# Second layer of a four-part network on one Trainium2 core: when a block's first sums are issued, when the residual is added, and where the picks' places are summed

## What is computed

```
x = x + _L0_attn_ref(_layernorm(x), ...)   # decayed attention, then a feed-forward
x = x + _L0_ffn_ref(_layernorm(x), ...)    # 2 shared and 16 routed experts, top 4
x = x + _L1_attn_ref(_layernorm(x), ...)   # selective scan: the part changed here
x = x + _L1_ffn_ref(_layernorm(x), ...)    # 2 x 32 experts, top 2 of each
```

```
def step(h, inp):
    x_t, dt_t, B_t = inp
    dA = jnp.exp(dt_t[:, :, None] * A[None])
    h = dA * h + dt_t[:, :, None] * B_t[:, None, :] * x_t[:, :, None]
    y_t = h.sum(-1) + D[None, :] * x_t
    return (h, y_t)
...
y = y * jax.nn.silu(res)
return y @ W_out.T
```

## Time and profile before

| what | value |
|---|---|
| median of 3 runs | 4823.72 us |
| the profiled execution's own time | 4822.83 us |
| its span, first to last instruction | 4821.0 us |
| first layer alone, to about | 2200 us |
| the scans of the second layer, from about | 2500 us |
| to about | 4145 us |
| a chunk of 64 scans, chunks 1 to 14 | 101.8 to 106.3 us |
| sorted experts, from about | 4207 us |

### The profile page before, as it was taken

One profiled execution on the slowest core, in us unless ns is written; L12 is line 12 of the kernel. 1 busy time (PEld: TensorE's weight loads), 2 busy tenths in 40 slices (PEclk: granted clock), 3 DMA queues, 4 the chain that ended last, 5 costly groups with the idle time before them and its releaser, 6 DMA issues. The chain is left out here.

```text
span 4821.0 us, 59211 instructions
## 1 busy us (share of the span) xinstructions
PE 4269.6 (89%) x19350; PEld 2845.4 (59%) x19350; DVE 3709.2 (77%) x5917; ACT 2521.4 (52%) x4939; POOL 3002.8 (62%) x1908
## 2 busy tenths in 40 slices
PE   5689999999999999998989988989989988599993
PEld 1345566555566555565656566666556666488883
DVE  6887777787778787776128999988999989555677
ACT  1343334344334344333458777777877777255552
POOL 3445545465545455554147888888888889655552
PEclk7899999999999999999999999999999999699997
DMA  4233323333333333332121122121122122596887
GB/s 145 83 105 105 110 88 104 107 104 107 108 96 97 110 99 112 105 102 85 54 85 49 67 78 99 71 74 67 71 82 99 69 69 71 180 254 196 266 278 279
DMA packets 304193, 545.54 MB, mean 113 GB/s; under 512 B 31504, under 2 KB 148496, under 8 KB 294928
## 3 DMA queue, kind: packets, MB, share of 16 engines
q1 hardware_dynamic: 275664, 465.56, 30.0%
q0 software_dynamic: 27648, 75.67, 4.4%
q10 hardware_dynamic: 576, 0.53, 0.1%
HBM read 422.72 MB, written 118.92 MB: 112 GB/s over the span
## 5 line engine op out<-in xcount | busy, mean ns | idle before, releaser
L1528 POOL TENSOR_TENSOR c_dbx<-c_dtx,c_Brep 128x1024 f32<-128x1024 f32 x512 | 1203.0, 2363 | 159.2 <-DVE c_hs L1546 119.0
L876 POOL TENSOR_TENSOR a_kv<-a_rk,a_kv 128x512 f32<-128x512 f32 x512 | 807.3, 1589 | 404.4 <-DMA a_kv<-v_rows 404.2
L1546 DVE TENSOR_TENSOR_SCAN c_hs<-psum,c_carry,c_dbx 128x512 f32<-128x512 f32 x768 | 934.6, 1263 | 56.3 <-ACT psum L1535 41.7
L885 DVE TENSOR_TENSOR_SCAN a_S<-a_decay,a_carry,a_kv 128x513 f32<-128x513 f32 x512 | 792.6, 1548 | 181.6 <-POOL a_kv L876 93.3
L802 POOL TENSOR_TENSOR a_hid_e<-a_hid_e,a_g_rep 128x512 f32<-128x512 f32 x256 | 387.1, 1514 | 772.7 <-ACT a_hid_e L791 590.4
L1535 ACT ACTIVATE psum<-c_dt,c_cols 128x512 f32<-128x512 f32 x1024 | 695.2, 688 | 285.6 <-DVE c_hs L1546 283.6
L1571 PEld LDWEIGHTS psum<-ident,c_hs 128*128 128x128 f32 x4096 | 491.9, 145 | 343.2 <-DVE c_hs L1546 169.7
L1571 PE MATMUL psum<-ident,c_hs 128*128 128x128 f32 x4096 | 596.6, 282 | 87.3 <-DVE c_hs L1546 85.1
L891 DVE TENSOR_TENSOR a_prod<-a_rk,a_S 128x512 f32<-128x512 f32 x512 | 546.4, 1067 | 71.9 <-PE psum L907 71.8
L783 PE MATMUL psum<-a_W_down,a_hid_e 128*128 128x256 f32 x2304 | 550.8, 385 | 54.0 <-POOL a_hid_e L802 29.7
L207 PE MATMUL psum<-a_xT,a_W_up 128*128 128x512 f32 x1152 | 559.5, 616 | 14.7 <-ACT a_hid_e L791 14.6
(11 more groups left out here) (287 smaller groups left out, 6817.4 us busy)
## 6 DMA issues: line engine op xcount, KB each, us to landing
a_kv<-v_rows SPq DMA_DIRECT2D x512, 256.0 KB
a_g_rep<-g_rows SPq DMA_DIRECT2D x256, 256.0 KB, 3.9
c_Brep<-b_rows SPq DMA_DIRECT2D x64, 1024.0 KB, 6.0
d_xs<-sorted_rows SPq DMA_DIRECT2D x320, 128.5 KB
d_w<-results SPq DMA_DIRECT2D x64, 512.0 KB, 11.4
d_w<-in_d_experts SPq DMA_DIRECT2D x32, 768.0 KB
a_xa<-in_L_attn_x SPq DMA_DIRECT2D x16, 512.0 KB, 4.7
v_rows<-a_rv SPq DMA_DIRECT2D x16, 512.0 KB, 3.0
```

Source lines behind the costliest of these rows:

```text
L876: m_kv[g] = pool.mark(nc.gpsimd.tensor_tensor(kv[:, g % NV, 1:C + 1], rk[slot][:, 1, hb, :], kv[:, g % NV, 1:C + 1], ALU.mult))
L885: m_scan[q] = dve.mark(nc.vector.tensor_tensor_scan(S[:, q % NS, :], decay[cq % 2][:, hb, :], kv[:, q % NV, :], carry[:, sq_:sq_ + 1], ALU ...
L1528: m_dbx[g] = m_dbx[g + 1] = pool.mark(nc.gpsimd.tensor_tensor(dbx[:, r:r + 2, :], dtx[slot][:, e, :].unsqueeze(1).broadcast_to([P, 2, C]), ...
L1546: m_scan[q] = dve.mark(nc.vector.tensor_tensor_scan(hs[:, q % NR, :], psum[:, DA + q % ND, :], dbx[:, q % NX, :], first, ALU.mult, ALU.add))
```

## The change

Three edits, all in `layer1_phase`.

1. The skip term of a block and the sums of its first state are no longer issued in the first state's step but, together with the second state's sums, one step later (`sum_up(q - 1)`, then `sum_up(q)`). What `background.pull()` puts into PE's queue in the step between now stands ahead of them.
2. The pause ahead of the residual's addition grows from `LAG + 2` to `LAG + 6`, 4 yields more, at 1.2 a step some three steps. All that follows in `after_scan` moves by as much, to some four or five steps where it crosses other pauses.
3. The places of the picks are reduced into the PSUM bank that holds the ranks, behind them (`in_room`), and the cast reads them there. The bank comes free with the cast (L1394), not with the multiplication (L1386). The tile `place` is gone.

```diff
-                yield from pause(LAG + 2)
+                yield from pause(LAG + 6)
...
-            ranks = bank[:, 0:TL * NE]
+            ranks, in_room = bank[:, 0:TL * NE], bank[:, TL * NE:TL * NE + TL * Z.picks]
...
-            m = G.freed[i] = dve.mark(nc.vector.tensor_tensor(
+            m = dve.mark(nc.vector.tensor_tensor(
                 at_pick[:, :, :, :], R["onehot"][:, :, :, :],
...
-            m = dve.mark(nc.vector.tensor_reduce(flat(place[:, :, :, :].rearrange("p t g k -> p t (g k)")), at_pick[:, :, :, :].rearrange("p r s e -> p (r s) e"), AX, ALU.add))
+            m = dve.mark(nc.vector.tensor_reduce(in_room, at_pick[:, :, :, :].rearrange("p r s e -> p (r s) e"), AX, ALU.add))
             yield
             dve.after(m)
-            m_done["placed", c] = [dve.mark(nc.vector.tensor_copy(flat(route.to_row[:, c % 2, :, :]), flat(place[:, :, :, :].rearrange("p t g k -> p t (g k)")))), m_xn]
+            m = G.freed[i] = dve.mark(nc.vector.tensor_copy(flat(route.to_row[:, c % 2, :, :]), in_room))
+            m_done["placed", c] = [m, m_xn]
...
+            def sum_up(q):
+
+                cq, sq = divmod(q, steps)
+                e, n = divmod(sq, N)
+                if n == 0:
+                    pe.after(m_done.get("y free"))
+                    for t in range(TL):
+                        nc.tensor.matmul(psum[:, YB, t * P:(t + 1) * P], xs[cq % 2][:, e, t * P:(t + 1) * P], skip_diag[:, e, :],
+                                         start=(t == 0), stop=False, skip_group_check=True)
+                pe.after(m_scan[q])
+                for t in range(TL):
+                    last = nc.tensor.matmul(psum[:, YB, t * P:(t + 1) * P], hs[:, q % NR, t * P:(t + 1) * P], ident[:, :],
+                                            is_transpose=True, start=False, stop=(n == N - 1 and t == TL - 1), skip_group_check=True)
+                m_sum[q] = pe.mark(last)
...
-                    if n == 0:
...
-                    m_sum[q] = pe.mark(last)
+                    for at in ((q - 1, q) if n == 1 else (q,) if n else ()):
+                        sum_up(at)
```

More of the change, by code:

```diff
@@ L1563, in scans @@
                         m_kept[q] = act.mark(nc.scalar.copy(carry[:, e, n - 3:n + 1], hs[:, r - 3:r + 1, C - 1]))
-                    if n == 0:
-                        pe.after(m_done.get("y free"))
-                        for t in range(TL):
-                            nc.tensor.matmul(psum[:, YB, t * P:(t + 1) * P], xs[cq % 2][:, e, t * P:(t + 1) * P], skip_diag[:, e, :],
-                                             start=(t == 0), stop=False, skip_group_check=True)
-                    pe.after(m_scan[q])
-                    for t in range(TL):
-                        last = nc.tensor.matmul(psum[:, YB, t * P:(t + 1) * P], hs[:, q % NR, t * P:(t + 1) * P], ident[:, :],
-                                                is_transpose=True, start=False, stop=(n == N - 1 and t == TL - 1), skip_group_check=True)
-                    m_sum[q] = pe.mark(last)
+                    for at in ((q - 1, q) if n == 1 else (q,) if n else ()):
+                        sum_up(at)
                     if sq == steps - 1:
@@ L1601, in layer1_phase @@
         at_pick = sb("at_pick", [P, TL * GR, TOP, EX])
-        place, over = sb("place", [P, TL, GR, TOP]), sb("over", [P, NE])
+        over = sb("over", [P, NE])
         R = router_buffers(nc, st, "c", GR, EX, TOP)
```

## The result

The changed kernel is slower: 4862.23 us in the median of six runs (4856.37 to 4866.02) against 4824.40 us for six runs of the kernel before. The ratio is 1.0075, with a 95% interval of 1.0062 to 1.0088. The forecast was 4823 us, 4804 to 4840. The time lies outside, on the side of the third rival and 17 us beyond it.

A forecast was written before the change was run, and what follows sets the result against it. The prediction took TensorE to bound the first stretch, with all engines near nine tenths busy. 14 x (-1.1 + 0.5 + 1.3) = +9.8 and -9.5 for the rest made +0.3 us: 4823 us, range 4804 to 4840.

The forecast's parts named there:

- the third rival: Rank matmuls behind the third gate wait start at 1.2 GHz, L1360 waits 2.1 us: slower, 4845 us; chance 0.25.
- What bounds the first stretch: Up to the first block's last sum TensorE is busy throughout; a 3.7 us wait replaces 3.25: +0.4 us a chunk.
- The first rival, the full gain: The removed wait ahead of L1309 is gained in full, with the casts' gain: 4751 us; chance 0.04.
- The 3.0 us of moved work and the 1.44 us ahead of scan 31: VectorE work moves behind the first gate multiplication, idle time ahead of scan 31 goes: both stretches -1.1 us a chunk.
- The third stretch, the table group: Later router work on VectorE no longer covers ScalarE's table group ahead of decay 45: +0.5 us a chunk.
- the cover I had priced: Router's small VectorE operations that hid ScalarE's table group ahead of decay 45; their loss: +0.5 us a chunk.
- L1360: VectorE waits for rank matmuls now behind the third gate wait: +1.3 us a chunk, between 0.6 and 2.1.
- Edit 1 at nothing: Skip term and first state's sums one step later: 0, since VectorE waits for none of the TensorE waits removed.
- Edit 3: 13 casts L1394 fall from 0.79 to 0.16 us each: -8.2 us in all, between 0 and -9.
- The 1.0 us that a PSUM source was to cost extra: Estimate from the Trainium skill's fixed cycles: 16 casts cost 1.0 us more, so the edit would bring 7.2.
- The slower rival: L1360 waits 2.1 us at the lower clock, the 1.44 us go only by half: 4845 us; chance 0.25.
- Chunk 15: Has no next chunk's products in the way and no idle time at L1309; only gets the new wait: +0.5 us.

The follow-up runs named there:

- router_later: The changed kernel with one more yield ahead of the router's product; ratio 1.0012 to the kernel before.
- filled: pause_alone with the four transposes ahead of the third block's skip term issued eight times over; ratio 1.0061 to the kernel before.
- pause_alone: The kernel before with only the residual's pause grown from LAG + 2 to LAG + 6; ratio 1.0127 to the kernel before.
- pause_plus5: The changed kernel with the residual's pause at LAG + 5 instead of LAG + 6; ratio 1.0050 to the kernel before.

## Why the prediction was wrong, step by step

- **What bounds the first stretch**: right. TensorE is busy throughout, the gate multiplication came at +25.45 in chunk 5, and the wait that took the removed one's place is there (4.34 us, forecast 3.7). The first rival, the full gain, fell with this.
- **The 3.0 us of moved work and the 1.44 us ahead of scan 31**: nearly right. First and second stretch gave -0.6 a chunk, not -1.1. The wait ahead of scan 31 went entirely; new waits ahead of scan 32 (4.1 us in all chunks) and of the second gate multiplication (2.5) took 0.5 of it back. Scan 34 comes behind that multiplication, in the third stretch.
- **The third stretch, the table group**: here is the step that failed. I costed the table groups by VectorE's cover alone, "+0.5 us a chunk, between 0 and 1.0". I let ScalarE's own queue stand as it was. The copies L1065 and the router's product are part of what moves; the copies cross the table group of L1173 and the product crosses a projection. I had looked for what VectorE waits for behind the moved instructions, not for what ScalarE and TensorE wait for. The term measured 2.6 us a chunk for my 0.5: the stretch grew by 1.4 where -0.7 was due. The waits add up to it: 13.8 us ahead of scan 39, 17.5 ahead of 45, 2.7 ahead of 46 and 2.4 more ahead of 34, together 36.4 / 14 = 2.6. `router_later` shows 1.6 of it to be the ring of waits, with TensorE at the lower clock in it; about 0.5 is the cover I had priced.
- **L1360**: the mechanism was right (`filled` shows the clock to be half of the wait in the order without edit 1), and edit 1 settles which end holds. The wait came to 0.9 us a chunk (0.5 in the median, 2.5 at most); I took 1.3. The 4.2 us of `pause_alone` belong to another order of TensorE's queue, for which I had given no figure. My 1.5 us for the lower clock was also loose: the lengths I gave make it 1.3 with one slow sum and 1.7 with two.
- **Edit 1 at nothing**: wrong in an instructive way. Alone it gains some 5 us. With the pause it saves 3 us a chunk at L1360, and it is what puts the router's product ahead of the skip term, which costs 1.8 ahead of scans 39 and 45: 2.2 in the changed kernel, 0.4 in `pause_alone`.
- **Edit 3**: -8.2 us forecast, -7.7 measured alone (-3 to -12). The agreement is in part luck: by the loop it is -13.5, more than all casts, and in the changed kernel 13 of the 16 casts are short from SBUF as well, while the edit is worth 10 us there. The 1.0 us that a PSUM source was to cost extra does not show: the casts take 0.15 us in the median from either memory when nothing delays them.
- **The slower rival** had the sign, the place at L1360 and the size within 17 us, but its cause was not the one that held. It got 0.25.

In the sum of the prediction, 14 x 2.35 = 33 us are missing, of which 29 lie between the second and the third gate multiplication. Chunk 15 came out 4.2 us better than forecast, and the parts ahead of the loop and behind it 6.9 us longer, which follows no edit.

## What to carry to other kernels

When a generator or a pause moves a piece of work, follow every instruction it issues on every engine, and ask of each what it now stands behind and what now stands behind it. The costly one may be a small copy that slips behind a table load. In a kernel whose engines are all at nine tenths, a wait in the list tells which work is late, not what is to be moved: moving the waiting instruction returned nothing, moving one piece of the work that stood ahead of the awaited one gained 1%, and moving three lost as much. Such a number of yields is to be swept on the chip, one by one: a single yield was worth 1%.

## What the runs showed of the hardware

- Useless matmuls made the program faster. 28 transposes more a chunk in a 3.8 us hole kept the granted clock at 1.00 where it had been 0.54, and took 32 us off the program by the ratios.
- Idle times of 1.07 and 1.15 us with 1.6 us of work between them left the skip term at 1.16 us; one of 3.77 us in a piece made it 2.07. Idle times of 0.64 and 1.60 us with 0.63 us of work between them were followed by a clock of 0.59 (`pause_plus5`, chunk 4).
- The long casts end with a GpSimd product. In the kernel before, chunk 7, VectorE's cast from SBUF to SBUF begins ahead of a product and ends 0.05 us behind it. All seven casts of that kernel over 0.3 us end 0.03 to 0.05 us behind a product. The same cast from PSUM never took over 0.175 us, in 144 instances:

```profile
3298.98 2.68 DVE L1394 CAST route_to_row<-c_place 128x16 int32<-128x16 f32 x1
...
3299.25 2.36 POOL L1528 TENSOR_TENSOR c_dbx<-c_dtx,c_Brep 128x1024 f32<-128x1024 f32 x1
```

The Trainium skill ("SBUF — State Buffer", "SBUF: two separate sides") says that VectorE in a two-port mode and GpSimd exclude each other for a whole instruction on a shared pair of ports. The two ends fit that, and the timing of the casts fits it too: moved by the pause to where no product of GpSimd runs, 13 of the 16 casts of `pause_alone` take 0.15 us from SBUF as well. Which of the two held the ports first in chunk 7 is not shown: the cast's record starts 0.27 us ahead of the product's, while GpSimd was still in an indirect DMA (L1475).
